# Pairwise field products on one core: waits left in place, a new table of stores, and loads closer to the stores around them

## What is computed

```python
vid = jnp.einsum('bfd,de->bfe', x, W)
idx_i, idx_j = jnp.triu_indices(32, k=1)
return x[:, idx_i, :] * vid[:, idx_j, :]      # 4096 x 496 x 64
```

## Time and profile before

| | before |
|---|---|
| median of 3 runs | 1291.55 us (1290.48 to 1291.65) |
| profiled execution, time and span | 1290.92 us, 1289.6 us |
| VectorE busy | 1086.8 us in 394 products |
| TensorE busy | 172.3 us, granted clock 0.569 of full |
| DMA | 553.75 MB, mean 429 GB/s |
| stores, loads | 73 and 8 |

### The profile page before, as it was taken

How to read it: one execution, slowest core, us unless ns; L and a number is a source line. 1 busy time by engine, 2 the same in 40 slices (tenths; PEclk the granted TensorE clock), 3 DMA queues, 4 the chain that set the end, 5 groups by cost and what they waited for, 6 DMA issues and landing times. The chain is left out here.

```text
span 1289.6 us, 1244 instructions
## 1 busy us (share of the span) xinstructions
PE 172.3 (13%) x256; PEld 67.0 (5%) x256; DVE 1086.8 (84%) x394; POOL 0.2 (0%) x4
## 2 busy tenths in 40 slices
PE   2011030301102030300020030303011030302000
PEld 1000010100001010100010010101000010101000
DVE  6499899699989899994337899898989898999970
POOL 0000000000000000000000000000000000000000
PEclk7557565555657565655565565656565565657555
DMA  9999999899999999999999999999999999999999
GB/s 407 437 421 443 424 437 429 378 431 431 439 431 423 423 455 423 439 437 413 430 417 439 432 432 439 431 435 427 439 437 425 451 427 423 451 427 423 450 427 392
DMA packets 11668, 553.75 MB, mean 429 GB/s; under 512 B 1296, under 2 KB 1296, under 8 KB 1296
## 3 DMA queue, kind: packets, MB, share of 16 engines
q1 hardware_dynamic: 10656, 520.10, 93.4%
q10 hardware_dynamic: 1008, 33.62, 6.1%
HBM read 33.62 MB, written 520.09 MB: 429 GB/s over the span
## 5 line engine op out<-in xcount | busy, mean ns | idle before, releaser
L195 DVE TENSOR_TENSOR mem<-mem,vid 128x1024 f32<-128x1024 f32 (+9 forms) x394 | 1086.8, 2834 | 163.8 <-DMA out_dram<-mem 128.1
L255 PE MATMUL vid<-mem 128*128 (+1 forms) x256 | 172.3, 837 | 1015.1 <-PEq L254 1015.1
L255 PEld LDWEIGHTS vid<-mem 128*128 128x128 f32 x256 | 67.0, 274 | 1119.6 <-issue 1119.6
L360 POOL MEMSET const-bfloat16-1.0<- 128x1 bf16 x1 | 0.1, 103 | 0.0
L360 POOL MEMSET const-uint8-127<- 128x1 uint8 x1 | 0.1, 103 | 0.0
L360 POOL MEMSET const-float32-1.0<- 128x1 f32 x1 | 0.1, 100 | 0.0
L360 POOL MEMSET const-float32-0.0<- 128x1 f32 x1 | 0.1, 99 | 0.2 <-issue 0.2
## 6 DMA issues: line engine op xcount, KB each, us to landing
out_dram<-mem SPq DMA_DIRECT2D x7, 6144.0 KB, 18.3
out_dram<-mem SPq DMA_DIRECT2D x6, 7168.0 KB, 20.4
out_dram<-mem SPq DMA_DIRECT2D x7, 5120.0 KB, 15.9
out_dram<-mem SPq DMA_DIRECT2D x5, 6656.0 KB, 19.8
out_dram<-mem SPq DMA_DIRECT2D x3, 7680.0 KB, 21.9
out_dram<-mem SPq DMA_DIRECT2D x3, 5632.0 KB, 17.0
out_dram<-mem SPq DMA_DIRECT2D x3, 4608.0 KB, 14.8
out_dram<-mem SPq DMA_DIRECT2D x2, 4096.0 KB, 14.7
```

What stands on the lines that cost most here:

```text
L195: self.engine.tensor_tensor(*operands, MULT).then_inc(self.dve, 1)
L255: nc.tensor.matmul(vid[:, b * BANK : b * BANK + BANK, :], lhsT=w, rhs=mem[:, bass.ds(k * step + (first + b * BANK), BANK), :], start=True, ...
L360: nc = _bacc.Bacc("TRN2", target_bir_lowering=False, num_devices=1, dynamic_dma_scratch_size=256)
```

## The change

It has three parts. `emit` now takes only VectorE's own wait off a product that has several waits; the waits for TensorE and for landings stay. `SLOTS` and `CUTS` are new: 75 stores in place of 73, and 367 products in place of 394, of the same 7,936 fields. The middle loads come behind store 37, which has 16 fields, and SyncE first waits for the landing of the store before it (36); the runs are 128, 114 and 14 fields in place of 128, 96 and 32, and the next store, 38, is held until the run of 114 has landed.

```diff
-STRETCHES = [(range(8, 16), [(128, 128), (32, 96), (0, 32)])]
+STRETCHES = [(range(8, 16), [(128, 128), (14, 114), (0, 14)])]
 SLOTS = [
...
+    (88, 32), (-96, 126), (64, 32), (56, 96), (64, 152), (80, 32), (88, 112), (96, 0), (-88,
+    128), (-80, 48), (48, 0), (88, 134), (-120, 14), (-120, 134), (112, 0), (120, 112),
+    (-104, 8), (-112, 151), (-128, 23), (-128, 158), (128, 0), (-128, 190), (-120, 31),
+    (128, 151), (128, 0), (-128, 210), (-120, 90), (88, 2), (-128, 222), (-80, 130), (-128,
+    0), (-128, 240), (112, 128), (-128, 0), (-120, 262), (128, 128), (-104, 16), (-16, 0),
+    (80, 360), (-104, 256), (80, 360), (40, 256), (-56, 296), (72, 368), (80, 256), (88,
+    336), (96, 224), (-88, 358), (-104, 254), (-88, 358), (88, 224), (104, 312), (112, 192),
...
-LOAD_BEHIND = [36]
+LOAD_BEHIND = [38]
...
             w = waits[k]
-            for s in sorted(w, key=lambda s: (s.name not in ("pe", "dve"), s.name)):
-                if len(w) == 1:
-                    break
+            if self.dve in w and len(w) > 1:
                 for b in range(k - 1, max(k - 6, earliest - 1), -1):
-                    if not waits[b].keys() - {s} and (s is not self.dve or w[s] <= b):
-                        waits[b][s] = w.pop(s)
+                    if not waits[b].keys() - {self.dve} and w[self.dve] <= b:
+                        waits[b][self.dve] = w.pop(self.dve)
                         break
...
                     tiles, runs = stretches.pop(0)
-                    held = stretch(sp, tiles, runs, f"g{slot}_")[-2], 16
+                    sp.after(stored[-2])
+                    landed = stretch(sp, tiles, runs, f"g{slot}_")[-2]
+                    held = (landed, 16) if len(runs) > 2 else (pe, tiles[0] * (F // BANK) + 1)
```

## The result

The changed kernel takes 1,286.26 us, the median of six runs (1,285.70 to 1,286.57), beside 1,291.53 (1,290.25 to 1,291.67) for the kernel before in the same series: ratio 0.9961, 95% interval 0.9948 to 0.9974. Predicted were 1,286.3, range 1,285.0 to 1,288.4. The profiled execution took 1,285.70, span 1,284.4, the span that the prediction's sum gives. The experiments will show that one of the two terms of that sum was right, and that the other is not seen at the end of the kernel.

What follows compares the result with a forecast made beforehand. The kernel was taken as a DMA stream, 1,276 us of a 1,289.6 us span. From the median of 1,291.55, 4.7 for the hole and 0.5 at the loads came off, 5.2 in all: 1,286.3 us, range 1,285.0 to 1,288.4.

Steps and rivals of the forecast that it cites:

- The hole: At 230 to 275 us, store 15 is issued late after a moved wait for TensorE; removing this gains 4.7 us.
- the rule of leads: Lead runs from a store's issue to the landing ahead; loss is 1.4 us less the lead, nothing from 1.4 on.
- The terms put at nothing: On VectorE, extra wait instructions for products left with two waits, and landing waits moved back, were costed at nothing.
- Part 2: New table of 75 stores and 367 products: adds no hole, lowest leads 3.3 and 3.5; VectorE's 2.4 us saving is hidden.
- part 1: Only VectorE's own waits are moved; store 15 would be issued at 247.1 with 4.1 us of lead, nothing lost.
- The turn-around: At the middle loads 1.5 us are lost; the edit could gain 1.5 and lose 0.7, taken as 0.5 gained.
- Rival A: The late load runs dry: 4.7 stays gained, the loads cost their 1.5 and 0.7 more; 1,287.6 us, chance 0.17.
- B: One boundary or product with two waits still makes a store late, by 4.7 us: 1,291.0 us, chance 0.08.
- C: 64 fields fail to cover TensorE at new-table boundaries, 3.8 us lost each; three give 1,297.8 us, chance 0.03.

Runs made afterwards that it cites:

- experiment 1: Kernel before, with its table and loads, and only the changed `emit` rule for the waits: 1,286.02 us, ratio 0.9962.
- experiment 3: Changed kernel with tile 3's wait for TensorE put back one product early, at the 64-field product: 1,290.19 us, ratio 0.9995.
- experiment 2: Changed kernel, new table and loads, but with the old rule for moving waits: 1,285.90 us, ratio 0.9963.
- Experiment 7: Changed kernel with the middle loads cut 128, 96, 32 in place of 128, 114, 14: 1,285.96 us, ratio 0.9961.
- experiment 8: Changed kernel with both edits at the loads undone, loads 128, 96, 32 and no wait for store 36's landing: 1,285.99 us, ratio 0.9963.
- experiment 10: Changed kernel with the middle loads cut 128, 64, 64: 1,286.18 us, ratio 0.9966.
- experiment 6: Changed kernel without SyncE's wait for store 36's landing before the first middle load: 1,286.02 us, ratio 0.9962.
- experiment 11: Changed kernel with the middle loads issued by ScalarE on its own DMA queue, same waits: 1,285.78 us, ratio 0.9961.
- Experiment 9: Kernel before, old table, with the new wait rule and middle loads cut 128, 114, 14: 1,286.46 us, ratio 0.9966.
- experiment 5: Changed kernel with store 38 held until the last load has landed, so it enters an empty queue: 1,287.34 us, ratio 0.9974.
- experiment 4: Changed kernel with SyncE waiting for store 37's landing too, so the first load enters an empty queue: 1,288.07 us, ratio 0.9977.

## Why the prediction was right, and where it was not

**The hole: right, in cause and in size.** The one wait for TensorE that the old rule put on tile 2's last product cost 4.7 us by the prediction, 4.7 by experiment 1, and the same fault elsewhere cost what the rule of leads gave (experiment 3). The terms put at nothing were rightly so: the changed kernel's trace has seven waits of VectorE that are instructions of their own, 21 ns each. VectorE's work fell by 1.2 us, half of the 2.4 forecast, which the stream hides either way. That the new table has no hole was right too: store 16 had the 3.8 of lead that were worked out, store 38 its 2.1, stores 48 and 51 3.4 and 3.5 for 3.3 and 3.5, and no store of the changed kernel was late.

**Part 2 is worth nothing beside part 1, as forecast.** The prediction gave the 4.7 to the rule and had the table only keep the leads; it did not say that the table by itself would cure the hole (experiment 2). Either would have given 1,286.

**The turn-around: no run shows the term of -0.5.** The prediction took the time lost at the landings around the loads for time lost at the end. By the landings the changed kernel did gain, about 0.6 us: 0.5 lost at the first load and nothing at the last, for 1.1 before. But three kernels that undo this edit whole or in part end at 1,286.0, as the rule alone does, for 1,286.3 of the changed kernel. Each against the kernel before of its own series, it is 5.3 for the changed kernel and 4.7 to 5.1 for these four. So the edit is worth something between 0.3 us lost and 0.6 gained at the end, and the runs can't tell which. By the mean of the 16 times, which one straggler moves little, nothing is gained at the loads (1.1 before, 1.2 after): about 1 us is lost there whether the load has 2.4 or 18 us of lead.

The windows seem to say that what is gained at the loads is lost again behind them: where the stretch at the loads has 419 to 422 GB/s (before, experiments 1, 7, 8 and 10), the 570 us behind it run at 434; where it has 425 to 428 (after, experiments 6 and 11), at 432 or 433. Experiment 9 has 422 and 433, experiment 2 416 and 434. One GB/s over that stretch is 1.3 us, too coarse to size this. The trace files say more. In the kernels whose last load has 32 or 64 fields, the stream behind the loads loses less by the mean (0.3 to 1.0 us, for 1.2 to 1.7 with 14 fields), but the kernel ends 0.9 to 1.5 us after the mean of the last store's 16 times, for 0.5 to 1.0. So the last of the 16, which ends the kernel, lacks much of what their mean is ahead. Why they drift apart is open.

**Why the number still came out.** In part by luck. The sum took 5.2 off the median of three runs, 1,291.55. The four series of the kernel before have medians from 1,290.71 to 1,291.53, so half a microsecond either way can't be seen in the end times, and a sum of 4.7 alone would have been borne out as well.

**Rival A** had a price for the late load, up to 0.7, which the runs do not bear out as one of its lead. Into an empty queue a load loses 2.8 by the landing, between the bounds of 1.4 and 3.1. But at a lead of 2.4 the first load lost anything from 0.0 to 2.0 by the landing, and with 18 us it lost 1.3 to 1.8 in four kernels and nothing in one. The late start did not decide the time. The fixed cost of 2.0 us, which the prediction took from the page "DMA: Bandwidth & Descriptors" of the Trainium skill (Anatomy of one DMA), is given there for DMAs that GpSimd issues; these are issued by SyncE, and experiment 5 has 1.4 for a store. Rivals B and C did not occur; experiment 3 brings B about by one wait, 1,290.2 for its 1,291.0.

## What to carry to other kernels

In a kernel that streams at full rate, work out for each transfer how long before the end of the one ahead it is issued; a stall costs only what exceeds that lead less the start-up time, so a 7 us stall can be free in one place and 4 us in another. When waits are moved to save wait instructions, never move one ahead past work that was to cover it. And change one part at a time: of this change of three parts one gains all of the time, a second would have gained it without the first, and the third looks useful in the landings only.

## What the runs showed that was not expected

A load into an empty queue costs 2.8 us by the landing before its data count, a store 1.4 (experiments 4 and 5). At the turn from stores to loads about 1 us is lost by the mean of the 16 times even with 18 us of lead (experiments 1, 6, 8 and 9). And a landing is the last of 16: with the same loads and leads, the changed kernel's first load loses 0.4 by it and that of experiment 2 2.0. Experiment 7 loses 1.6 us at its last load, where the changed kernel loses nothing; its median is 0.3 us lower, its profiled execution 0.5 us longer. So a loss of a microsecond between two landings of one execution is no ground yet for a gain at the end.
